# A depthwise convolution that reads its rows from PSUM, its halo through ScalarE's bias, and norm rows transposed at other places

## The chip, the core and the metric

The kernel runs on one core of a Trainium2 chip. Five engines work beside each other: TensorE (PE, with its weight loads shown as PEld), VectorE (DVE), ScalarE (ACT), GpSimd (POOL), and SyncE (SP), which here issues the DMAs. The metric is the device time of one execution in microseconds. Before the change three runs took 3058.79, 3064.16 and 3069.94 us; the median is 3064.16.

## The reference

One "macaron" block over x of 4 x 1024 tokens and 512 channels, all in float32: half a feed-forward layer, a Mamba mixer, half a feed-forward layer. Each of the three reads a layer norm of the running x.

```python
x = x + 0.5 * ffn(layernorm(x))          # (silu(g*gate_s) * (u*up_s)) @ down.T * down_s, 1408 wide
x = x + mixer(layernorm(x))
x = x + 0.5 * ffn(layernorm(x))

# the mixer: 1024 inner channels, 16 states, a convolution of 4 taps
h, gate = split(x @ W_in.T)
h = silu(causal_depthwise_conv4(h) + conv_b)
ts, B, C = split(h @ Wx.T)               # 128 + 16 + 16 columns, each with an rms norm
delta = softplus(ts @ Wdt.T + dt_bias)
s_t = exp(delta_t * A) * s_(t-1) + delta_t * B_t * u_t       # scan over time, u = h
y = (s_t . C_t + D * u) * silu(gate)
out = y @ Wout.T
```

## The kernel before

The 4096 tokens are cut into eight chunks of 512; two chunks make a sequence of 1024, so an odd chunk continues the even one before it and needs its last three columns (the halo) for the convolution. A chunk goes through stages: `ffn1`, `prep_in` (input projection, convolution, gates, x projection), `dt0` to `dt3` (each two of eight channel tiles of delta), `post` (gating and output projection) and `ffn2`. Beside them `scan` runs 32 groups a chunk, each of a GpSimd product (line 1020), four exponentials on ScalarE into PSUM (1034), four scans on VectorE (1043), 16 transposes on TensorE (1060) and four accumulations, on VectorE (1071) or through ScalarE and GpSimd (1075, 1078).

Float32 products run in split form (`hi` and `lo` parts, `PARTS`): three products for each, or two where the weight has no `lo` part. The program holds both forms of the feed-forward weights' order and picks one by a flag that it works out at the start; with these ternary weights the shorter one runs. A stage begins with `make_xT`, which transposes the 512 x 512 norm rows, loaded by DMA into `xnb`, through four PSUM banks into `xT`; ScalarE writes `hi` (527) and VectorE `lo` (528). PSUM has four banks `pm` for all stages, two `pa` for the exponentials, two `pt` for the scan's transposes.

In `prep_in` each of the eight channel tiles has a product of 12 matmuls (505) into a bank. ScalarE copies it into a row of `xnb` (738), behind three halo columns (736, odd chunks), and writes the last tap with bias to `a` (740); in even chunks it saves the last three columns (745). VectorE adds the three other taps (750), ScalarE takes the tanh (700), VectorE makes u (701), ScalarE its `hi` (704), GpSimd its `lo` (706). Two tiles are open at a time: a tile's 700 to 706 are issued behind the taps of the next. A gate product (12 matmuls, ScalarE tanh 785, VectorE 787) stands between. Two of the four banks are held from the start for the x projection, of which 12 matmuls (`x_step`, 720) follow each tile with a lag of two. `x_proj` then normalises the result on ScalarE and GpSimd, and `dt0` transposes it.

The order of stages is a table: `OPENING` for the first, then `ROUND` for each chunk, where `LAG` = 3 puts `post` and `ffn2` three chunks later. No engine's order is written by hand. Each stage issues into streams ("threads": M for stages, C for the convolution, D for softplus, S and T for the scan, L for norms); `merge` (from line 114) plays all streams against a cost model (`span`: for VectorE 0.09 + n/960 us, and the `more` that an operation gives) with ranks by engine, and takes at each step the instruction that can start first. The result is a fixed order on each engine, and an instruction waits on semaphores in that order. Softplus works in three buffers, `spx`, `spe`, `spw`, which one part must leave (918 and the stores) before the next part's biased copy (882) may write.

## Time and profile before

| | |
|---|---|
| profiled execution, its own time | 3060.28 us |
| its span, first to last instruction | 3058.5 us |
| busy: TensorE, VectorE, ScalarE, GpSimd | 80%, 85%, 58%, 75% of the span |
| granted TensorE clock, mean | 0.885 |
| first and last scan start | 205.7 and 2939.0 us |
| VectorE taps of the convolution (750) | 192 instructions |
| VectorE's last step of the convolution (701) | 64 instructions |

The shares are means over stages with different limits, so the stretch of the scans and single stages are read beside them. A duration in the trace holds whatever an instruction waits for after its issue; an idle gap before it is listed apart with what ended it. Lines in the rows are those of the kernel before.

### The profile page before, as it was taken

Reading aid. Unit: us, or ns where it says so; the run is one execution under the profiler, and the core shown is the slowest. Engines: PE = TensorE matmul, PEld = TensorE weight load, DVE = VectorE, ACT = ScalarE, POOL = GpSimd, SP = SyncE. Lnnn points to the kernel's source line nnn. Section 1 sums busy time; section 2 is a strip of 40 time slices with the busy share of each in tenths; the row PEclk is TensorE's granted clock in tenths of the full one; section 3 lists DMA queues with packets and bytes.
Section 4 is the critical chain, followed back from the end, with each engine's and each line's share of the span. In section 5 each row is a group of like instructions: output and inputs, shape, how many; then the busy total and the mean of one; then the engine's idle time right before and its main releaser. Section 6 shows DMA issues by size and latency. Waiting matters only on the chain. (4 is left out here: it accounts for less than half of the span.)

```text
span 3058.5 us, 37435 instructions
## 1 busy us (share of the span) xinstructions
PE 2454.4 (80%) x12266; PEld 1985.8 (65%) x12266; DVE 2595.8 (85%) x3097; ACT 1778.5 (58%) x3029; POOL 2288.8 (75%) x1348
## 2 busy tenths in 40 slices
PE   7568786876878899779987899778988897697768
PEld 5456565655657678567766677667766675576646
DVE  5449897999899889799998899899998897899962
ACT  5456557666646656657665656646656656745421
POOL 2237758886986689768996789858897698997832
PEclk9778797988888899889989999889989897897879
DMA  7544653564376566865577466855677475575624
GB/s 271 198 160 137 198 195 90 176 226 160 128 265 233 170 208 220 290 206 171 187 258 285 145 203 221 272 191 172 208 238 274 132 238 191 194 250 191 199 79 133
DMA packets 294953, 608.70 MB, mean 199 GB/s; under 512 B 23008, under 2 KB 23776, under 8 KB 294752
## 3 DMA queue, kind: packets, MB, share of 16 engines
q1 hardware_dynamic: 294752, 606.23, 59.8%
q8 instruction: 101, 1.65, 0.2%
q14 instruction: 100, 0.82, 0.1%
HBM read 453.57 MB, written 152.57 MB: 198 GB/s over the span
## 5 line engine op out<-in xcount | busy, mean ns | idle before, releaser
L1020 POOL TENSOR_TENSOR sbuf<-dus,bring 128x1024 f32<-128x1024 f32 x512 | 1236.0, 2430 | 271.1 <-PE pt L1060 150.2
L505 PE MATMUL pm<-xT,wring 128*128 128x512 f32 x4352 | 1144.9, 412 | 92.3 <-DVE xT L528 48.7
L505 PEld LDWEIGHTS pm<-xT,wring 128*128 128x128 f32 x4352 | 825.2, 196 | 263.1 <-issue 92.9
L1034 ACT ACTIVATE pa<-dls,cst 128x512 f32<-128x512 f32 x1024 | 692.0, 688 | 475.4 <-DVE sbuf L1043 453.9
L1060 PE MATMUL pt<-ident,sbuf 128*128 128x128 f32 x4096 | 688.2, 309 | 314.6 <-DVE sbuf L1043 188.9
L1060 PEld LDWEIGHTS pt<-ident,sbuf 128*128 128x128 f32 x4096 | 538.4, 158 | 484.4 <-DVE sbuf L1043 242.0
L1043 DVE TENSOR_TENSOR_SCAN sbuf<-pa,carry,sbuf 128x512 f32<-128x512 f32 x512 | 634.4, 1270 | 37.4 <-ACT pa L1034 23.7
L1043 DVE TENSOR_TENSOR_SCAN sbuf<-pa,sbuf 128x512 f32<-128x512 f32 x512 | 607.4, 1211 | 65.8 <-ACT pa L1034 58.3
L1071 DVE SCALAR_TENSOR_TENSOR acc<-pt,cT,acc 128x512 f32<-128x512 f32 x768 | 548.6, 742 | 98.6 <-PE pt L1060 86.3
L577 PE MATMUL pm<-wring,act 128*128 128x512 f32 x2176 | 589.1, 414 | 32.6 <-DVE hd L957 23.4
L577 PEld LDWEIGHTS pm<-wring,act 128*128 128x128 f32 x2176 | 405.5, 195 | 122.9 <-DVE hd L957 26.6
L528 POOL TENSOR_TENSOR act<-hd,act 128x512 fp32r<-128x512 f32 x240 | 310.3, 1299 | 105.5 <-ACT act L527 104.9
L1078 POOL TENSOR_TENSOR acc<-acc,tmp 128x512 f32<-128x512 f32 x192 | 253.1, 1318 | 72.7 <-ACT tmp L1075 72.6
L640 ACT ACTIVATE th<-pm,csh 128x512 f32<-128x512 f32 x176 | 120.5, 685 | 160.4 <-PE pm L505 159.9
L706 POOL TENSOR_TENSOR act<-hd,act 128x512 fp32r<-128x512 f32 x64 | 82.2, 1284 | 154.1 <-ACT act L704 151.5
L750 DVE SCALAR_TENSOR_TENSOR aa<-xnb,csh,aa 128x511 f32<-128x511 f32 (+1 forms) x144 | 179.8, 1249 | 16.2 <-ACT aa L740 15.2
L527 ACT ACTIVATE act<-hd 128x512 fp32r<-128x512 f32 x240 | 148.8, 623 | 56.6 <-DVE hd L957 40.9
L1075 ACT ACTIVATE tmp<-pt,cT 128x512 f32<-128x512 f32 x192 | 131.2, 683 | 66.4 <-POOL acc L1078 59.2
L644 DVE SCALAR_TENSOR_TENSOR aa<-th,pm 128x512 f32<-128x512 f32 x176 | 118.3, 672 | 53.0 <-ACT th L640 52.4
L720 PE MATMUL pm<-wxs,act 128*128 128x160 f32 x768 | 121.1, 312 | 51.5 <-POOL act L706 37.3
L720 PEld LDWEIGHTS pm<-wxs,act 128*128 128x128 f32 x768 | 113.7, 226 | 61.0 <-issue 22.5
L652 DVE SCALAR_TENSOR_TENSOR hd<-aa,csh,pm 128x512 f32<-128x512 f32 x176 | 129.7, 737 | 14.3 <-PE pm L505 11.5
(121 smaller groups left out, 2106.5 us busy)
## 6 DMA issues: line engine op xcount, KB each, us to landing
wring<-wsp SPq DMA_DIRECT2D x408, 512.0 KB, 4.4
bring<-b_d SPq DMA_DIRECT2D x256, 256.0 KB, 3.9
xn_d<-tb SPq DMA_DIRECT2D x24, 1024.0 KB, 8.9
xnb<-xn_d SPq DMA_DIRECT2D x21, 1024.0 KB, 6.5
x_d<-tb SPq DMA_DIRECT2D x16, 1024.0 KB, 5.8
u_d<-hd SPq DMA_DIRECT2D x64, 256.0 KB, 2.3
sg_d<-hd SPq DMA_DIRECT2D x64, 256.0 KB, 2.9
tb<-x_d SPq DMA_DIRECT2D x16, 1024.0 KB, 6.7
```

What stands on the lines that cost most here:

```text
L505: f = lambda e, pw=pw, px=px, k=k, first=(i == 1), end=(i == total): e.matmul(pm[b][:, 0:n], lhs(pw, k), rhs(px, k), start=first, stop=end)
L527: t_hi = M.op(hi_eng, lambda e: e.activation(hi, b_or_src, ACT.Copy), t_src, *waits)
L528: t_lo = M.op(lo_eng, lambda e: e.tensor_tensor(lo, b_or_src, hi, ALU.subtract), t_hi)
L577: f = lambda e, b=b, pw=pw + half, px=px, k=k, tt=tt, slot=slot, start=(i and k == 0), stop=(end and k == nk - 1): e.matmul(pm[b][:, :], a ...
L720: f = lambda e, b=b, tt=tt, pw=pw, px=px, start=first_here, stop=(end and k == NI - 1): e.matmul(pm[b][:, (tt % 2) * XW:(tt % 2 + 1) * XW] ...
L750: t_c = C.op("dve", lambda e, xb=xb, a=a, k=k, lo=lo, cw=cw: e.scalar_tensor_tensor(a[:, lo:TC], xb[:, HALO - k + lo:HALO - k + TC], cw(3 ...
L1020: t_p = S.op("pool", lambda e, s2=s2, s3=s3, h=h: e.tensor_tensor(sbuf[:, s3, h * m:(h + 1) * m, :], dus[:, h * m:(h + 1) * m, :], bring[: ...
L1034: t_e = S.op("act", lambda e, k=k, i=i, pb=pb, n=n: e.activation(pa[pb][:, :], dls[:, k, :], ACT.Exp, scale=col(C_A + i * N + n)), dl_tok[ ...
L1043: t_sc = S.op("dve", lambda e, d=d, pb=pb, init=init: e.tensor_tensor_scan(d, pa[pb][:, :], d, init, ALU.mult, ALU.add), t_e, t_ps[k], *(s ...
L1060: f = lambda e, tt=tt, k=k, s3=s3, pb=pb: e.matmul(pt[pb][:, k * P:(k + 1) * P], sbuf[:, s3, k, tt * P:(tt + 1) * P], ident[:, :], is_tran ...
L1071: f = lambda e, tt=tt, a=a, c=c, pb=pb, n=n: e.scalar_tensor_tensor(a, pt[pb][:, :], cT[:, c % 4, tt, n:n + 1], a, ALU.mult, ALU.add)
L1078: t_a = T.op("pool", lambda e, a=a: e.tensor_tensor(a, a, tmp[:, 0, :], ALU.add), t_s, *w)
```

## The change

Names and tables first. `ROUND` has `dt2` in front of `post` and `dt3` in front of `prep_in`; `INSIDE` puts `dt1` into the middle of `ffn1`; `EARLY` names the stages that transpose the next stage's rows.

```diff
+EARLY = ("ffn","prep_in")
+D_ACT = 5
+CLOSE_NOW = tuple(range(8))
+INSIDE = (("ffn1", "dt1"),)
+TWO_OPEN = (0,)
+WITH_CONV = (0,)
-ROUND = (("ffn1",0),("dt1",1),("post",LAG),("dt2",1),("prep_in",0),("dt3",1),("ffn2",LAG),("dt0",0))
+ROUND = (("ffn1",0),("dt1",1),("dt2",1),("post",LAG),("dt3",1),("prep_in",0),("ffn2",LAG),("dt0",0))
```

Chunk 0 keeps rows in `xnb` (`rows`), two open tiles and x steps between tiles. Chunks 1 to 7 leave the product in its bank: the taps read the bank at a shifted start, and the tanh goes back into it. The halo's part of the first three columns of an odd chunk, with the convolution's bias, is worked out for all tiles by six small GpSimd products and sums (`hfix`), and enters as the bias of three ScalarE activations of one column. Each tile is finished before the next is issued.

```diff
+                if not even:
+                    cw4 = csh[:, H_CW:H_CW + 4 * NI].rearrange("p (i k) -> p i k", k=4)
+                    at = {3: 0, 2: 4, 1: 6}
+                    for k in (3, 2, 1):
+                        t_fix = C.op("pool", lambda e, k=k: e.tensor_tensor(
+                            hfix[:, :, at[k]:at[k] + k], hsave[:, :, HALO - k:HALO],
+                            cw4[:, :, 3 - k:4 - k].broadcast_to([P, NI, k]), ALU.mult),
+                            *(hs_tok if k == 3 else ()), *freed("hfix"), n=8)
...
-                    t_th = C.op("act", lambda e: e.activation(xb[:, HALO:HALO + TC], a, ACT.Tanh), t_c, table="tanh")
+                    h = x_buf[i % 3] if rows else pm[b][:, :]
+                    t_th = C.op("act", lambda e: e.activation(h, a, ACT.Tanh), t_c, table="tanh")
                     t_u = C.op("dve", lambda e: e.scalar_tensor_tensor(
-                        hd[:, r, :], xb[:, HALO:HALO + TC], 1.0, a, ALU.add, ALU.mult), t_th, *freed(("hd", r)))
+                        hd[:, r, :], h, 1.0, a, ALU.add, ALU.mult), t_th, *freed(("hd", r)), more=0.2 if rows else 0.0)
...
+                    x = x_buf[i % 3] if rows else pm[b][:, :]
+                    if rows:
+                        C.op("act", lambda e, b=b, x=x: e.activation(x, pm[b][:, :], ACT.Copy), t, *x_free[i % 3])
                     if even:
...
+                        hs_tok[i] = C.op("dve", lambda e, b=b, i=i: e.tensor_copy(
+                            hsave[:, i, 0:HALO], pm[b][:, TC - HALO:TC]), t_c, *freed("hsave"), n=1)
+                    else:
+                        for k in range(HALO):
+                            C.op("act", lambda e, b=b, a=a, i=i, k=k, cw=cw: e.activation(
+                                a[:, k:k + 1], pm[b][:, k:k + 1], ACT.Identity, bias=hfix[:, i, k:k + 1],
+                                scale=cw(3)), t, t_fix, *freed(a_key[i % 3]), n=40)
+                        t_c = C.op("act", lambda e, b=b, a=a, i=i, cw=cw: e.activation(
+                            a[:, HALO:TC], pm[b][:, HALO:TC], ACT.Identity, bias=hc(H_CB + i), scale=cw(3)),
+                            t, more=0.1)
...
                     for k in range(1, 4):
-                        lo = k if even else 0
-                        t_c = C.op("dve", lambda e, xb=xb, a=a, k=k, lo=lo, cw=cw: e.scalar_tensor_tensor(
-                            a[:, lo:TC], xb[:, HALO - k + lo:HALO - k + TC], cw(3 - k), a[:, lo:TC], ALU.mult, ALU.add),
-                            t_c, more=0.06)
+                        t_c = C.op("dve", lambda e, x=x, a=a, k=k, cw=cw: e.scalar_tensor_tensor(
+                            a[:, k:TC], x[:, 0:TC - k], cw(3 - k), a[:, k:TC], ALU.mult, ALU.add),
+                            t_c, more=0.3 if rows else 0.06)
                     if opened:
                         finish()
-                    opened.append((i, r, t_c))
+                    opened.append((i, r, b, t_c))
+                    if c not in TWO_OPEN:
+                        finish()
```

In chunks 1 to 7 the banks of the x projection are taken behind the last gate, seven x steps follow, then the next stage's transposes, then the last x step and `x_proj`. `ffn` calls `next_xT` in front of its down-projection; it acts where the next stage but the dt parts is one whose norm rows are stored by then, and loads and transposes them.

```diff
+            def next_xT(where):
+
+                key = following[0]
+                if where in EARLY and key in ln_out:
+                    need_xn(key)
+                    early_xT[key] = make_xT(xn_tok.pop(key))
+                    prefetch()
...
+                    if j == J // 2 and within:
+                        within()
                 finish()
                 free["xT"] = (t,)
+                if not first:
+                    next_xT("ffn")
...
+                if c not in WITH_CONV:
+                    x_banks()
+                for k in range(NI - XLAG if c in WITH_CONV else 0, NI - 1):
                     x_step(k)
-                free["act"] = (x_done[-1][1],)
-                x_proj(c, x_done)
+
+                if c:
+                    next_xT("prep_in")
+
+                def close():
+                    x_step(NI - 1)
+                    free["act"] = (x_done[-1][1],)
+                    x_proj(c, x_done)
+
+                to_close.append(close)
+                if c in CLOSE_NOW:
+                    close_x()
```

Three places show how the orders move. Lines in the pieces of the change are its own: 809 for 750, 766 for 701, 869 for 787, 1127 for 1043, 1155 for 1071, 743 for 720, 512 for 505, 520 for 513, 584 for 577, 1144 for 1060. A scan stands as SCALAR_TENSOR_TENSOR `sbuf<-pa`.

VectorE in `prep_in` of chunk 5, from the taps of one tile to the last step of another, before:

```order
L750 SCALAR_TENSOR_TENSOR th<-xnb,csh,th 128x512 x2
L1071 SCALAR_TENSOR_TENSOR acc<-pt,cT,acc 128x512
L750 SCALAR_TENSOR_TENSOR th<-xnb,csh,th 128x512
L701 SCALAR_TENSOR_TENSOR hd<-xnb,aa 128x512
L1071 SCALAR_TENSOR_TENSOR acc<-pt,cT,acc 128x512 x2
L1043 SCALAR_TENSOR_TENSOR sbuf<-pa,sbuf 128x512
L787 SCALAR_TENSOR_TENSOR hd<-th,pm 128x512
```

and of the change, one tile:

```order
L809 SCALAR_TENSOR_TENSOR th<-pm,csh,th 128x511
L869 SCALAR_TENSOR_TENSOR hd<-th,pm 128x512
L809 SCALAR_TENSOR_TENSOR th<-pm,csh,th 128x510
L1127 SCALAR_TENSOR_TENSOR sbuf<-pa,sbuf 128x512
L809 SCALAR_TENSOR_TENSOR th<-pm,csh,th 128x509
L1127 SCALAR_TENSOR_TENSOR sbuf<-pa,sbuf 128x512 x2
L766 SCALAR_TENSOR_TENSOR hd<-pm,th 128x512
L1127 SCALAR_TENSOR_TENSOR sbuf<-pa,sbuf 128x512
```

Before, a tile's last step (701, on `aa`) stands behind the three taps of the next tile (on `th`); now it stands behind its own, with scans between, and its first tensor is the bank `pm`.

TensorE at the end of `prep_in` of chunk 5, where `xT,wring` are the last gate products, `wxs` the x projection, `tsT` dt parts and `ident,xnb` the transposes of the next stage, `ffn2`, before:

```order
L1060 MATMUL pt<-ident,sbuf 128x128 x8
L505 MATMUL pm<-xT,wring 128x512 x6
L1060 MATMUL pt<-ident,sbuf 128x128 x4
L505 MATMUL pm<-xT,wring 128x512
L1060 MATMUL pt<-ident,sbuf 128x128 x4
L720 MATMUL pm<-wxs,act 128x160 x24
L1060 MATMUL pt<-ident,sbuf 128x128 x12
L505 MATMUL pm<-tsT,wdts 128x512
L1060 MATMUL pt<-ident,sbuf 128x128 x4
L505 MATMUL pm<-tsT,wdts 128x512 x5
L513 MATMUL pm<-ident,xnb 128x128 x16
L505 MATMUL pm<-xT,wring 128x512 x9
```

and of the change:

```order
L743 MATMUL pm<-wxs,act 128x160 x6
L1144 MATMUL pt<-ident,sbuf 128x128 x4
L743 MATMUL pm<-wxs,act 128x160
L1144 MATMUL pt<-ident,sbuf 128x128 x4
L743 MATMUL pm<-wxs,act 128x160 x44
L520 MATMUL pm<-ident,xnb 128x128 x2
L1144 MATMUL pt<-ident,sbuf 128x128 x8
L520 MATMUL pm<-ident,xnb 128x128 x6
L1144 MATMUL pt<-ident,sbuf 128x128 x8
L520 MATMUL pm<-ident,xnb 128x128 x8
L743 MATMUL pm<-wxs,act 128x160 x12
L512 MATMUL pm<-xT,wring 128x512 x3
```

The x projection stood in twelves between the products and now stands behind them in one piece; the transposes moved in front of its last twelve and the first product of `ffn2` follows these.

TensorE at the end of `ffn2` of chunk 2 (`wring,act` is the down-projection, `ident,ssb` and `tsT` are `dt0`), before:

```order
L1060 MATMUL pt<-ident,sbuf 128x128 x4
L577 MATMUL pm<-wring,act 128x512 x17
L513 MATMUL pm<-ident,ssb 128x128 x4
L513 MATMUL pm<-ident,bn 128x128
L1060 MATMUL pt<-ident,sbuf 128x128 x8
L505 MATMUL pm<-tsT,wdts 128x512 x3
L1060 MATMUL pt<-ident,sbuf 128x128 x4
L505 MATMUL pm<-tsT,wdts 128x512
L1060 MATMUL pt<-ident,sbuf 128x128 x4
L505 MATMUL pm<-tsT,wdts 128x512 x2
L513 MATMUL pm<-ident,xnb 128x128 x16
L505 MATMUL pm<-xT,wring 128x512 x10
```

and of the change:

```order
L512 MATMUL pm<-xT,wring 128x512 x4
L520 MATMUL pm<-ident,xnb 128x128 x2
L1144 MATMUL pt<-ident,sbuf 128x128 x4
L520 MATMUL pm<-ident,xnb 128x128 x2
L1144 MATMUL pt<-ident,sbuf 128x128 x4
L520 MATMUL pm<-ident,xnb 128x128 x12
L584 MATMUL pm<-wring,act 128x512 x20
L1144 MATMUL pt<-ident,sbuf 128x128 x8
```

The 16 transposes of `ffn1`'s rows stood behind `dt0`, right in front of the products that need them; they now stand in front of the down-projection.

## Rows read from the trace of the kernel before

**Rows 1.** the page, busy time by engine, share of the span, instructions

```profile
PE 2454.4 (80%) x12266; PEld 1985.8 (65%) x12266; DVE 2595.8 (85%) x3097; ACT 1778.5 (58%) x3029; POOL 2288.8 (75%) x1348
```

**Rows 2.** windows: us, busy PE, PEld, DVE, ACT, POOL, PEclk, DMA share, GB/s

```profile
230.00:2945.00 2715.00, 2212.28 (x11235) 1787.66 (x11235) 2449.86 (x2842) 1643.73 (x2788) 2198.29 (x1267) 0.89 0.61 201
```

**Rows 3.** windows of one round's ffn1 and prep_in

```profile
1132.50:1218.80 86.30, 81.78 (x437) 67.22 (x437) 80.27 (x96) 55.94 (x95) 81.75 (x47) 1.00 0.63 207
...
1271.20:1386.30 115.10, 91.08 (x472) 75.63 (x471) 106.20 (x120) 74.85 (x143) 79.80 (x47) 0.89 0.63 207
```

**Rows 4.** waits: engine, line, releaser: us in total, times, longest

```profile
ACT act L704 <- DVE hd L701: 119.9, 48, 8.7
...
DVE acc L1071 <- PE pt L1060: 86.3, 89, 5.4
...
PE pm L505 <- DVE xT L528: 48.7, 21, 4.7
...
PE pm L505 <- DVE hd L787: 33.1, 12, 7.9
```

**Rows 5.** groups by line on VectorE: busy us, mean ns, idle before

```profile
L1071 DVE SCALAR_TENSOR_TENSOR acc<-pt,cT,acc 128x512 f32<-128x512 f32 x768 | 548.6, 742 | 98.6 <-PE pt L1060 86.3 <-POOL acc L1078 6.8 <-ACT acc L1067 0.8
...
L750 DVE SCALAR_TENSOR_TENSOR aa<-xnb,csh,aa 128x511 f32<-128x511 f32 (+1 forms) x144 | 179.8, 1249 | 16.2 <-ACT aa L740 15.2
...
L750 DVE SCALAR_TENSOR_TENSOR th<-xnb,csh,th 128x512 f32<-128x512 f32 (+3 forms) x48 | 57.5, 1198 | 8.2 <-ACT th L740 7.7
...
L701 DVE SCALAR_TENSOR_TENSOR hd<-xnb,aa 128x512 f32<-128x512 f32 x48 | 51.3, 1068 | 1.3 <-ACT xnb L700 1.2
...
L787 DVE SCALAR_TENSOR_TENSOR hd<-th,pm 128x512 f32<-128x512 f32 x64 | 42.9, 670 | 15.9 <-DMA sg_d<-hd 10.9 <-ACT th L785 4.8
...
L701 DVE SCALAR_TENSOR_TENSOR hd<-xnb,th 128x512 f32<-128x512 f32 x16 | 15.2, 951 | 0.0
```

**Rows 6.** lines 750 and 1071: duration ns min/median/max

```profile
L750 DVE SCALAR_TENSOR_TENSOR aa<-xnb,csh,aa x144: 718/752/2927, 110.6 to 2401.8; 128x512 f32<-128x512 f32 x72, 128x511 f32<-128x511 f32 x24, 128x510 f32<-128x510 f32 x24, 128x509 f32<-128x509 f32 x24
...
L1071 DVE SCALAR_TENSOR_TENSOR acc<-pt,cT,acc x768: 717/743/758, 232.2 to 2944.3; 128x512 f32<-128x512 f32 x192
```

**Rows 7.** timeline of GpSimd: start us, us

```profile
1359.08 2.37 POOL L1020 TENSOR_TENSOR sbuf<-dus,bring 128x1024 f32<-128x1024 f32 x1
```

**Rows 8.** timeline of VectorE beside it

```profile
1359.28 2.71 DVE L750 SCALAR_TENSOR_TENSOR aa<-xnb,csh,aa 128x511 f32<-128x511 f32 x1
1361.92 1.27 DVE L1043 TENSOR_TENSOR_SCAN sbuf<-pa,carry,sbuf 128x512 f32<-128x512 f32 x1
1363.11 0.72 DVE L750 SCALAR_TENSOR_TENSOR aa<-xnb,csh,aa 128x510 f32<-128x510 f32 x1
```

**Rows 9.** groups by line on ScalarE and GpSimd

```profile
L738 ACT ACTIVATE xnb<-pm 128x512 f32<-128x512 f32 x64 | 37.4, 584 | 15.1 <-PE pm L505 15.1
L740 ACT ACTIVATE aa<-pm,csh 128x512 f32<-128x512 f32 x48 | 37.0, 771 | 0.0
...
L736 ACT ACTIVATE xnb<-hsave 128x3 f32<-128x3 f32 x32 | 6.2, 194 | 0.0
...
L825 POOL TENSOR_TENSOR cT<-ssb,rr 128x64 f32<-128x64 f32 x8 | 2.4, 298 | 0.0
```

**Rows 10.** timeline of TensorE, two x steps

```profile
1041.24 2.81 PE L720 MATMUL pm<-wxs,act 128*128 128x160 f32 x24
```

**Rows 11.** timeline of ScalarE, dt0 and ffn1, then one tile in prep_in

```profile
1137.87 0.67 ACT L882 ACTIVATE spx<-pm,cst 128x512 f32<-128x512 f32 x1
...
1166.78 0.67 ACT L640 ACTIVATE th<-pm,csh 128x512 f32<-128x512 f32 x1
...
1288.24 0.76 ACT L740 ACTIVATE aa<-pm,csh 128x512 f32<-128x512 f32 x1
...
1304.86 0.63 ACT L704 ACTIVATE act<-hd 128x512 fp32r<-128x512 f32 x1 [5.49 <-DVE hd L701]
```

**Rows 12.** timeline of GpSimd, dt0's last product

```profile
1169.25 2.40 POOL L918 TENSOR_TENSOR spw<-spx,spw 128x1024 f32<-128x1024 f32 x1
```

More of the change, by code:

```diff
@@ L240, in macaron @@
         hsave = sb("hsave", [P, NI, 4])
+        hfix = sb("hfix", [P, NI, 8])
         cst = sb("cst", [P, NCONST])
@@ L680, in prep_in @@
                 even = c % 2 == 0
-                src, t_in = (tb, first_xn[-1]) if c == 0 else (xnb, xn_tok.pop((1, c)))
-                t_xT = make_xT(t_in, src)
+                t_xT = ready_xT((1, c)) if c else make_xT(first_xn[-1], tb)
                 if c + 1 < NCH:
                     pre_norm(free, ln_out, c + 1)
+                if c == 0 and c not in WITH_CONV:
+                    prefetch(0)
                 u_tok, g_tok = [], []
-                opened, x_ready_of = [], {}
-                xbanks = [bank() for h in range(2)]
@@ new lines, in prep_in, with x_banks, x_step @@
+                opened, x_ready_of, x_done, xbanks = [], {}, [], []
+                def x_banks():
+                    xbanks.extend(bank() for h in range(2))
+                    held.update(b for b, w in xbanks)
+                def x_step(k):
+                    for tt in range(4):
+                        b, w = xbanks[tt // 2]
+                        for pw, px in PARTS:
+                            begins, ends = (pw, px) == PARTS[0], (pw, px) == PARTS[-1]
+                            opens = begins and k == 0 and tt % 2 == 0
+                            f = lambda e, b=b, tt=tt, pw=pw, px=px, start=opens, stop=(ends and k == NI - 1): e.matmul(
+                                pm[b][:, (tt % 2) * XW:(tt % 2 + 1) * XW], act[:, pw, k, tt * P:(tt + 1) * P],
+                                wxs[:, px, k, :], start=start, stop=stop, skip_group_check=True)
+                            ws = (*x_ready_of[k], t_small[0]) if begins and tt == 0 else ()
+                            t = M.matmul(f, *ws, *(w if opens else ()), n=XW, last=ends and tt % 2 == 1)
+                            if ends and k == NI - 1 and tt % 2 == 1:
+                                x_done.append((b, t))
@@ L711, in finish @@
                     x_ready_of[i] = t_hi, t_lo
[L713 to L728 removed]
                 for i in range(NI):
[L730 removed]
+                    r, a = i % 2, a_buf[i % 3]
                     slot, t_w = piece(WIN + i)
@@ L762, in prep_in @@
-                prefetch(0 if c == 0 else 1)
+                if opened:
+                    finish()
+                if rows:
+                    free["xnb"] = tuple(t for f in x_free for t in f)
+                    prefetch(0)
                 if c:
@@ L839, in dt0 @@
             def dt0(c):
+                close_x()
                 t_bn, t_ct, t_ss = bn_tok[c]
@@ L1169, in build @@
                     scan(c)
-                if kind in KIND and (kind, c) not in INPLACE:
+                if kind in KIND and (kind, c) not in INPLACE and (KIND[kind], c) not in early_xT:
                     need_xn((KIND[kind], c))
-                stage[kind](c)
+                later = [x for x in order[order.index((kind, c)) + 1:] if x[0][:2] != "dt"]
+                following[0] = None
+                if later and later[0][0] in KIND and later[0] not in INPLACE:
+                    following[0] = KIND[later[0][0]], later[0][1]
+                more = [lambda k=k, n=n: stage[k](n) for k, n in [inner.get((kind, c))] if k] if (kind, c) in inner else []
+                stage[kind](c, *more)
         build(True, True)
```

91 lines of the change are left out of this document (49 added, 42 removed).

## The prediction, made before the changed kernel was run

> **What bounds the kernel now.** I read five views, from wide to narrow. First the busy times: VectorE leads with 2595.8 us of the span, TensorE and GpSimd follow at 80% and 75% [rows 1]. Then the long middle stretch alone, from 230 us to 2945 us, in which the scans run: VectorE is busy 2449.86 us of 2715, that is 90.2%, GpSimd 2198.29 (81.0%), TensorE 2212.28 (81.5%), ScalarE 61% [rows 2]. VectorE's idle time there is 265 us. Third, two stages of one round of the main chain: in ffn1 TensorE is busy 81.78 of 86.3 us, but in prep_in VectorE is busy 106.20 of 115.1 us and TensorE only 91.08 [rows 3]. So ffn stages are close to TensorE's limit, and prep_in, the one the change rewrites, is close to VectorE's. Fourth, the waits: ScalarE's operand split waits 119.9 us for VectorE's last convolution step, and the accumulation behind the scan waits 86.3 us for TensorE [rows 4]. Last the instruction groups of the convolution: they run on VectorE at 1249, 1198, 1068 and 951 ns, while a like instruction with its first tensor in PSUM takes 670 to 742 ns [rows 5, 6].
>
> Why they differ is seen in one pair of rows. A GpSimd product runs from 1359.08 to 1361.45 [rows 7]; a VectorE convolution step issued at 1359.28 takes 2.71 us and ends at 1361.99, half a microsecond after it, where the next one, with GpSimd idle, takes 0.72 [rows 8]. The spread over the whole run says the same: least 718, median 752, longest 2927 ns; the accumulation that reads PSUM stays between 717 and 758 in 768 executions [rows 6]. The step reads two SBUF tensors, the accumulation one.
>
> **The change part by part.** The profiled execution took 3060.28 us, 1.8 us more than its span, and lies 3.9 us under the median of the runs shown; I count from 3060.
>
> *Convolution out of PSUM (chunks 1 to 7).* 192 steps of L750 cost 179.8 + 57.5 = 237.3 us [rows 5]; seven eighths of them, 168, cost 207.6. At the 742 ns of L1071, which has the same operands (PSUM tensor, scalar column, SBUF tensor), they cost 124.7: 82.9 us less. L701's 64 cost 51.3 + 15.2 = 66.5; 56 of them 58.2; at the 670 ns of L787 [rows 5] 37.5: 20.7 less. The 32 saves of the last three columns move from ScalarE to VectorE; for so small a copy the nearest row is ScalarE's 194 ns for three columns [rows 9]: 6.2 us more. VectorE loses 97 us of work. Bounds for the new steps: 717 to 758 ns [rows 6], so 95 to 102.
>
> That the bank is now read several times has a rule against it: the Trainium skill ("VectorE: DVE Perf Modes", "Rules for kernel authors") advises copying a matmul's result to SBUF first when many operations follow, and its errata table charges 120 cycles for a PSUM source against 58 for SBUF. By that each of the 224 operations would cost 65 ns more, 14.5 us in all (an estimate from that page). The trace does not bear it out: the least times are 717 ns with PSUM and 718 without [rows 6].
>
> *ScalarE.* 56 copies of L738 go (584 ns, 32.7 us), with 32 halo copies (6.2) and the 32 saves; 96 one-column activations come, at the 194 ns of the three-column copy [rows 9] 18.6 us. At least 20 us less on an engine that is busy 61% of the stretch: worth nothing by itself. GpSimd gets 24 tiny products for the halo, at most 8 us at the 298 ns of the kernel's 64-element products [rows 9], ahead of the convolution and in its gaps: nothing.
>
> *Banks and order in prep_in.* Two of the four pm banks no longer are held for the x projection while tiles run, so conv and gate products rotate over four; TensorE's 33.1 us of waits for L787 [rows 4], which frees a gate's bank, shrink. Against it, a bank is held through the tile's whole chain, and each tile is finished before the next begins: the overlap of two open tiles goes. All x steps stand behind the last tile. 24 of them took 2.81 us [rows 10], so 96 take 11.2 us at the end of the stage, 84 in one run and 12 behind the next stage's transposes, with VectorE left to the scans.
>
> *Norm rows early.* A stage's first product waits for the split of its transposed rows: 48.7 us in 21 waits, 2.3 each [rows 4]. The change does this early at the end of prep_in for chunks 1 to 7 and in front of the down-projection of ffn2 for four chunks: 11 starts, 25 us of TensorE waits at most. Its waits are half filled by other streams, so none to 25.
>
> *dt1 inside ffn1 (five rounds).* Its biased copy L882 may not overwrite spx before dt0's L918 has read it. dt0's copy began at 1137.87 and L918 ended at 1169.25 + 2.40 = 1171.65; ffn1's sixth tanh, behind which dt1 now stands, began at 1166.78 [rows 11, 12], and its product is done some 3 us later. With the stage's start 3 us earlier the wait is 0 to 5 us, ScalarE's queue behind it (the scan's exponentials) waiting too: 0 to 25 us in five rounds, I take 10.
>
> *The sum.* What does 97 us less on VectorE give? If its 265 us of idle time stay as they are, 97. The idle time should grow a little: TensorE's work is unchanged, and its 2212 us would then be 84.5% of 2618. The scans fill VectorE whenever they are free to, as the stretch shows, and at the end of the kernel little else is left for it; the shorter prep_in lets them run ahead of the main chain. I take 80%, 78 us, and add 12 for the early transposes (half of 25) less 10 for dt1: 80 us. 3060 - 80 = **2980 us**. Own range of this case: 70% to 110% of 97 with the ends of the other terms, 2950 to 3015.
>
> **The rivals.** *TensorE and GpSimd take over:* the gain of prep_in returns as waits in the ffn stages, where TensorE is at 81.78 of 86.3 [rows 3]. Only prep_in's own idle can be won: its 115.1 us cannot fall below TensorE's 91, and other stages grow by the scan work pushed into them. A third of the 97 remains: 3060 - 32 = 3028. For it: TensorE's 81.5%. Against: no engine but VectorE passes 82% over the stretch.
>
> *More than the sum:* waits go together with work (prep_in's copies, the bank waits, 48.7 us of split waits), and idle falls below 265 by a third of the split and bank waits' 82 us and a few more: 97 + 33, 2930. For it: the convolution's 2 us stalls are not foreseen by the planner, whose price for a step is 0.09 + 512/960 + 0.06 = 0.68 us (line 73 and the `more` of line 750), and the new 0.74 fits it.
>
> *Slower, by the tile's chain:* one tile at a time costs the biased copy 0.77 [rows 9] + three columns 0.6 + three steps 2.23 + tanh 0.63, as the split [rows 11] + last step 0.67 + split 0.63 = 5.5 us; if each of the four VectorE steps finds a scan (1.27 [rows 8]) and an accumulation (0.74) in front, 8 more, and six handovers 1: 14.5 us. Eight tiles and the x run are 127 us against 115.1, five to seven times: 12 x 7 = 84 us on the main chain; 3060 + 84 - 25 = about 3120. It decides from 13 us a tile on. For it: the first tile's copy began at 1288.24 and its split only at 1304.86, 16.6 us later [rows 11]. Against: much of that was the second tile's work queued between.
>
> *No change:* the excess over 0.72 us is not the second SBUF tensor's, and stays. Then only the small terms act, +10 to -15: 3055. Against it: [rows 6 to 8]. By the page's table above (the Trainium skill, "VectorE: DVE Perf Modes") 14.5 would come on top.
>
> **How the numbers follow.** Less than 0.3%, 9 us, cannot be told from no change: the three runs differ by 11. Forecast 56%, take-over 19%, more 12%, slower 8%, no change 5%. The range 2925 to 3045 holds the first two and most of the third, 84%. Faster: 56 + 19 + 12, less 1 for the edge of the take-over: 86%. Same 6%, slower 8%.
>
> **What would show it.** The steps and L701's successor at 740 and 670 ns with no tail past 800; VectorE near 2500 us; prep_in at 95 to 105 us; waits of the split for the last step nearly gone; waits for xT under 25 us. Wrong: steps still in the microsecond, a prep_in over 115 us, L882 waiting for L918 by several us a round, or VectorE lighter by 97 us with the span unmoved.

## The result, and the profile after

The changed kernel took 3032.21 us (median of 4 runs, 3031.36 to 3035.97), the kernel before 3063.3 beside it: a ratio of 0.9899, 95% interval 0.9883 to 0.9914. It is 31 us faster; 80 were forecast.

The page of the kernel after, busy time by engine as in [rows 1]; then the taps of the convolution on VectorE and its last step, least, median and longest duration, as in [rows 6]:

```profile
PE 2454.4 (81%) x12266; PEld 1988.6 (66%) x12266; DVE 2487.0 (82%) x3129; ACT 1769.5 (58%) x3005; POOL 2262.2 (75%) x1372
```

```profile
L809 DVE SCALAR_TENSOR_TENSOR aa<-pm,csh,aa x126: 718/737/751, 378.8 to 2411.6; 128x511 f32<-128x511 f32 x42, 128x510 f32<-128x510 f32 x42, 128x509 f32<-128x509 f32 x42
L809 DVE SCALAR_TENSOR_TENSOR th<-pm,csh,th x42: 719/734/750, 400.8 to 2392.9; 128x511 f32<-128x511 f32 x14, 128x510 f32<-128x510 f32 x14, 128x509 f32<-128x509 f32 x14
L766 DVE SCALAR_TENSOR_TENSOR hd<-pm,aa x42: 657/667/692, 385.5 to 2414.5; 128x512 f32<-128x512 f32 x42
L766 DVE SCALAR_TENSOR_TENSOR hd<-pm,th x14: 660/666/683, 406.4 to 2395.5; 128x512 f32<-128x512 f32 x14
```

The work went as priced: 2595.8 to 2487.0 is 108.8 us less on VectorE (97 forecast), the taps stand at 734 to 737 ns with nothing past 751, the last step at 667. The time did not follow. Windows of the middle stretch, and of one round's ffn1 and prep_in (us, busy PE, PEld, DVE, ACT, POOL, then clock, DMA share, GB/s), answering to [rows 2, 3]:

```profile
230.00:2915.00 2685.00, 2214.79 (x11247) 1792.92 (x11247) 2341.00 (x2866) 1634.88 (x2772) 2168.64 (x1283) 0.89 0.60 202
...
1155.80:1242.60 86.80, 79.99 (x395) 64.04 (x394) 64.42 (x79) 55.34 (x85) 71.93 (x42) 0.98 0.73 249
1298.00:1415.60 117.60, 93.89 (x503) 77.10 (x501) 109.88 (x150) 74.33 (x116) 84.97 (x58) 0.88 0.63 211
```

The two stages are bounded as in [rows 3]: ffn1 from the transposes of dt0 to its last product, prep_in from the dt part in front of it to its last product or transpose. VectorE now idles 344 us of the stretch (265 of a like one before). prep_in takes 117.6 us, where 95 to 105 were expected and over 115 was to be the sign of being wrong, and VectorE is 93% busy in it (92% before). ffn1 is as long as before (86.3), with TensorE busy 79.99 us of it, and VectorE has fallen from 80.27 to 64.42. The scans alone in the same two windows (us, busy VectorE, count), before and after, show where they went, from ffn1 into prep_in:

```profile
1132.50:1218.80 86.30, 45.23 (x38) 1.00 0.63 207
1271.20:1386.30 115.10, 45.29 (x37) 0.89 0.63 207
```

```profile
1155.80:1242.60 86.80, 32.32 (x27) 0.98 0.73 249
1298.00:1415.60 117.60, 53.62 (x43) 0.88 0.63 211
```

The waits, as in [rows 4], two of the kernel before that stand in no row yet, then those of the kernel after:

```profile
POOL sbuf L1020 <- PE pt L1060: 150.2, 58, 8.5
...
DVE sbuf L1043 <- POOL sbuf L1020: 20.2, 8, 5.8
```

```profile
POOL sbuf L1104 <- PE pt L1144: 229.2, 81, 9.5
...
DVE sbuf L1127 <- POOL sbuf L1104: 73.7, 30, 8.8
...
PE pm L512 <- DVE xT L535: 30.4, 13, 3.8
...
ACT act L773 <- DVE hd L766: 21.8, 16, 2.5
```

ScalarE's split waits 21.8 us for the last step (119.9 before), but the scan's own loop waits more: GpSimd's product 229.2 us for TensorE's transposes (150.2 before), and VectorE's scan 73.7 for that product (20.2).

What ended last has changed too. VectorE's timeline (start, duration) at the last scan, before and after, and beside them pieces of the chain of work that ended last:

```profile
2939.05 1.27 DVE L1043 TENSOR_TENSOR_SCAN sbuf<-pa,carry,sbuf 128x512 f32<-128x512 f32 x1
...
2939.13 1.20 DVE sbuf L1043
2940.38 3.09 PE pt L1060 x12
```

```profile
2894.40 2.45 DVE L1127 TENSOR_TENSOR_SCAN sbuf<-pa,carry,sbuf 128x512 f32<-128x512 f32 x2
...
2900.03 7.99 PE pm L584 x35
...
2908.40 4.43 DMA act<-u_d
...
2914.11 8.40 DMA act<-u_d
...
2924.14 18.01 PE pm L584 x78
```

The scans end 43 us earlier, the kernel only 29 us earlier in its span: behind the last scan stood 118 us (3058.5 - 2940.3), just the last half of post and the last ffn2; now it is 133. Before, the chain runs through the last scan and its transposes: the stages waited for the scans at the end. After, it runs from a down-projection (584) over loads of post into the last ffn2, past the scans: the stages are late by themselves, by some 15 us. This stretch behind the last scan tells the two cases apart in every run: it is 117 to 119 us where the scans end last (before, e1 to e4, e7, e10, e12, e13, e15 to e17) and 133 to 176 where the stages do (after, e5, e6, e8, e9, e11, e14, e18).

From the first scan to the end of the last, before and after, the columns of the windows above:

```profile
205.69:2940.32 2734.63, 2223.32 (x11267) 1795.96 (x11267) 2460.89 (x2852) 1654.87 (x2806) 2214.29 (x1273) 0.89 0.61 201
```

```profile
207.15:2896.85 2689.70, 2213.18 (x11211) 1790.51 (x11212) 2344.14 (x2864) 1643.56 (x2786) 2176.31 (x1283) 0.89 0.60 201
```

VectorE has 117 us less to do there and idles 72 us more. The scans have come closer to their data, too. GpSimd's last product of dt1 and the first of the scan, chunk 7, before and after:

```profile
2576.94 2.40 POOL L918 TENSOR_TENSOR spw<-spx,spw 128x1024 f32<-128x1024 f32 x1
...
2670.95 4.77 POOL L1020 TENSOR_TENSOR sbuf<-dus,bring 128x1024 f32<-128x1024 f32 x2 [1.57 <-DMA dus<-du_d]
```

```profile
2575.99 2.36 POOL L1001 TENSOR_TENSOR spw<-spx,spw 128x1024 f32<-128x1024 f32 x1
...
2610.77 4.65 POOL L1104 TENSOR_TENSOR sbuf<-dus,bring 128x1024 f32<-128x1024 f32 x2 [4.68 <-DMA dus<-du_d]
```

The scan starts 92 us behind its data before, 32 after.

The seven tile sections of prep_in (first tap of a chunk to its last, chunks 1 to 7) say why. Each "sum" row gives their length and the busy times over them, the second one that of the scans alone. Before:

```profile
sum 554.00, PE 433.44 PEld 354.83 DVE 527.71 ACT 308.13 POOL 357.01; mean PE 61.92 PEld 50.69 DVE 75.39 ACT 44.02 POOL 51.00
...
sum 554.00, DVE 180.28; mean DVE 25.75
```

After:

```profile
sum 537.90, PE 422.66 PEld 330.21 DVE 496.42 ACT 339.65 POOL 396.76; mean PE 60.38 PEld 47.17 DVE 70.92 ACT 48.52 POOL 56.68
...
sum 537.90, DVE 228.54; mean DVE 32.65
```

VectorE lost 104 us of convolution here, but its busy time fell only by 31: scans (48 us more) and their accumulations (25 more) took the room. The sections hardly got shorter, 76.9 us each instead of 79.1. VectorE's timeline in one tile after shows how:

```profile
1354.80 0.74 DVE L809 SCALAR_TENSOR_TENSOR aa<-pm,csh,aa 128x511 f32<-128x511 f32 x1
1355.46 1.27 DVE L1127 TENSOR_TENSOR_SCAN sbuf<-pa,carry,sbuf 128x512 f32<-128x512 f32 x1
1356.65 0.73 DVE L809 SCALAR_TENSOR_TENSOR aa<-pm,csh,aa 128x510 f32<-128x510 f32 x1
1357.29 1.27 DVE L1127 TENSOR_TENSOR_SCAN sbuf<-pa,carry,sbuf 128x512 f32<-128x512 f32 x1
1358.48 0.72 DVE L809 SCALAR_TENSOR_TENSOR aa<-pm,csh,aa 128x509 f32<-128x509 f32 x1
```

A scan stands behind each of the first two taps. The timeline has 112 pairs of neighbouring taps of one tile in chunks 1 to 7: 11 stand side by side, and between the others are 58 scans, 35 accumulations and some steps of the stages.

### The profile page after: what moved, and what is told of

Same layout as the page of the kernel before. It is cut to its first block and busy times, and to the rows that moved or that the text cites. A ratio compares the mean times of both kernels' runs of the same rounds, so it can differ in the third digit from the quotient of the medians.

```text
span 3029.6 us, 37464 instructions
## 1 busy us (share of the span) xinstructions
PE 2454.4 (81%) x12266; PEld 1988.6 (66%) x12266; DVE 2487.0 (82%) x3129; ACT 1769.5 (58%) x3005; POOL 2262.2 (75%) x1372
## 5 line engine op out<-in xcount | busy, mean ns | idle before, releaser
L1104 POOL TENSOR_TENSOR sbuf<-dus,bring 128x1024 f32<-128x1024 f32 x512 | 1219.1, 2395 | 314.6 <-PE pt L1144 229.2
L512 PE MATMUL pm<-xT,wring 128*128 128x512 f32 x4352 | 1132.5, 409 | 89.2 <-DVE xT L535 30.4
L1144 PE MATMUL pt<-ident,sbuf 128*128 128x128 f32 x4096 | 678.3, 306 | 263.4 <-DVE sbuf L1127 154.2
L1144 PEld LDWEIGHTS pt<-ident,sbuf 128*128 128x128 f32 x4096 | 532.1, 157 | 424.4 <-DVE sbuf L1127 204.5
L600 POOL TENSOR_TENSOR tb<-tb 128x512 f32<-128x512 f32 x64 | 80.7, 1294 | 64.5 <-DVE tb L598 64.5
```

What stands on the lines that cost most here:

```text
L512: f = lambda e, pw=pw, px=px, k=k, first=(i == 1), end=(i == total): e.matmul(pm[b][:, 0:n], lhs(pw, k), rhs(px, k), start=first, stop=end)
L1104: t_p = S.op("pool", lambda e, s2=s2, s3=s3, h=h: e.tensor_tensor(sbuf[:, s3, h * m:(h + 1) * m, :], dus[:, h * m:(h + 1) * m, :], bring[: ...
L1144: f = lambda e, tt=tt, k=k, s3=s3, pb=pb: e.matmul(pt[pb][:, k * P:(k + 1) * P], sbuf[:, s3, k, tt * P:(tt + 1) * P], ident[:, :], is_tran ...
```

## The experiments

Theory M: two chains, the stages and the scans, share VectorE in one fixed order; the end is set by the later, and the gain is only what that one gets. Rivals: T, TensorE and GpSimd are the limit of the ffn stages; S, the scans wait for their data; O, accidents of the planner's order. All are the changed kernel with the edit shown, unless said otherwise.

**Parts undone, and who gives way.**

e1, the convolution from SBUF rows in all chunks, two tiles open, the x projection's banks held and its steps between the tiles as before; the rest of the change stays. The lines left out place the loads of norm rows and free the banks to suit.

```diff
-TWO_OPEN = (0,)
-WITH_CONV = (0,)
+TWO_OPEN = tuple(range(8))
+WITH_CONV = tuple(range(8))
...
```

> The changed kernel with the convolution of all chunks out of SBUF rows again, two tiles open and x steps between the tiles; early transposes, halo bias and dt order stay. Theory M (main chain): the freed VectorE time of the change went to scan steps between a tile's taps, so the chain of stages got no shorter, and now it, no longer the scan, ends last. VectorE gets back about 100 us; the scan ends last again: 3050 to 3065 us. Theory T (TensorE and GpSimd at their throughput): the PSUM form is worth about its third, 30 us: also 3050 to 3065. If the PSUM form is worth nothing and early transposes and dt order made the whole gain: 3030 to 3038.

3060.38 us, ratio 0.9997 (0.998 to 1.0015): with VectorE at 2593.5 us again, nothing is left of the gain. M and T had named the same range, so the run does not part them. The new order of dt and the early rows are in it, and together are worth nothing beside SBUF rows.

e2, dt1 to dt3 at their old places.

```diff
-INSIDE = (("ffn1", "dt1"),)
+INSIDE = ()
-ROUND = (("ffn1",0),("dt1",1),("dt2",1),("post",LAG),("dt3",1),("prep_in",0),("ffn2",LAG),("dt0",0))
+ROUND = (("ffn1",0),("dt1",1),("post",LAG),("dt2",1),("prep_in",0),("dt3",1),("ffn2",LAG),("dt0",0))
```

> The changed kernel with the table of stages of before (post between dt1 and dt2, dt3 behind prep_in) and dt1 not inside ffn1. M: a scan's data come 20 to 50 us later a chunk, but post follows with no dt work in front; as the stages end last, 3005 to 3030 us, with the first post behind the last prep_in 15 to 30 us earlier. If the scan's supply is what counts: 3045 to 3065. T: no change, 3027 to 3037.

3054.93 us, 0.998 (0.996 to 1.0). VectorE has the light load (2478.5), yet 23 us are lost. M's 3005 to 3030 is missed, and the rival that the scan's supply counts (3045 to 3065) is right. GpSimd's waits in this run show that the scan stands for its data (43.4 us in the kernel after, 71.5 before):

```profile
POOL sbuf L1104 <- DMA dus<-du_d: 99.5, 18, 14.6
```

So the order of dt1 to dt3, of which I had priced dt1 alone, at a loss of 10, is a gain of 23 beside PSUM.

e3, two tiles open in all chunks, everything else as changed.

```diff
-TWO_OPEN = (0,)
+TWO_OPEN = tuple(range(8))
```

> The changed kernel with two convolution tiles open in all chunks (a tile's tanh and last step issued behind the next tile's taps), still out of PSUM. M: the tile section of prep_in falls from 76 to 80 us to 65 to 72, and the time by 10 to 40 us: 2992 to 3022. T: no change, 3027 to 3037. If the tile's own chain is not what holds prep_in but VectorE's queue: section and time unchanged too.

3008.79 us, 0.9827 (0.9809 to 0.9845), a time within what M said: one tile at a time costs 23 us. But M's reason is not borne out: a section takes 75.5 us, not 65 to 72. The scans end last again, 6 us earlier than as changed, and the stretch behind them is 117 us instead of 133.

e4, scans and accumulations give way to the stages on VectorE.

```diff
-"t": dict(pe=0, dve=3, ...  "s": dict(act=4, dve=4,
+"t": dict(pe=0, dve=50, ... "s": dict(act=4, dve=60,
```

> The changed kernel with a handicap in the planner: on VectorE a scan is placed only where it can start 0.6 us before any other work that is ready, an accumulation 0.5 us (ranks 60 and 50 in place of 4 and 3). Same instructions, other order. M: taps follow each other without scans between, the tile section falls from 76 to 80 us to about 60 and the time by 30 to 70 us: 2960 to 3000. T: TensorE's and GpSimd's work is the same, so 3025 to 3040 whatever prep_in does.

3072.81 us, 1.0037 (1.0023 to 1.0051): slower, M's and T's numbers missed. The sections are what the forecast had wanted:

```profile
sum 418.70, PE 353.13 PEld 282.01 DVE 363.52 ACT 272.87 POOL 278.19; mean PE 50.45 PEld 40.29 DVE 51.93 ACT 38.98 POOL 39.74
...
sum 418.70, DVE 123.73; mean DVE 17.68
```

59.8 us a section. The last chunk's prep_in begins at 2195.9 us instead of 2336.1, but the scans left undone end last:

```profile
2959.15 1.28 DVE L1127 TENSOR_TENSOR_SCAN sbuf<-pa,carry,sbuf 128x512 f32<-128x512 f32 x1
```

**Which chain is late.**

e5, no early transposes: `EARLY = ()`.

> The changed kernel with EARLY = (): every stage transposes its own rows at its start, as before. The prediction's price (half of 25 us): 3032 + 12 = 3044 us, waits of TensorE for xT back at 45 to 50 us. Theory M (two chains, the stages and the scans, share VectorE in a fixed order, and the end is set by the later of the two; behind the change the stages are the later one by some 15 us): the wait lies on the later chain, 3038 to 3050. Theory T (TensorE and GpSimd are the limit of the ffn stages, VectorE's gain is lost there): a wait of TensorE counts in full, 3045 to 3057.

3035.37 us, 0.9897 (0.9881 to 0.9914), close to the change's own 0.9899: the early rows are worth 3 us or nothing; all three numbers missed. TensorE's waits for xT, expected at 45 to 50 us, rose from 30.4 only to 34.4, so the run takes little of them back.

e6, from chunk 2 on the scan reads the chunk before's delta, delta*u, B and C.

```diff
-                d_tok, (t_b,), t_ct = scan_ready[c]
+                d = c - 1 if c > 1 else c
+                d_tok, (t_b,), t_ct = scan_ready[d]
...
-dls[:, k, :], dl_d[c, 4 * ig + k]
+dls[:, k, :], dl_d[d, 4 * ig + k]
...
```

> The changed kernel, but from chunk 2 on the scan reads delta, delta*u, B and C of the chunk before, so it never waits for this chunk's softplus; all work and all traffic stay, only the numbers differ. Theory S (the shorter convolution has let the scans catch up with their data, and now they wait for softplus: scan(7) starts 29 us behind its data, 117 before the change): the scans end at least 30 us earlier and the time is 2985 to 3015 us. Theory M: the scans end earlier, but they stand in front of the stages' steps on VectorE, and the stages end last: 3020 to 3045. Theory T: 3025 to 3035, nothing moves.

3025.56 us, 0.9865 (0.9846 to 0.9884). The last scan:

```profile
2846.89 1.27 DVE L1128 TENSOR_TENSOR_SCAN sbuf<-pa,carry,sbuf 128x512 f32<-128x512 f32 x1
```

The scans end 49 us earlier and the kernel is 7 us faster. So the scans did wait for their data, as S says, but S's time falls: behind the change the stages are the later chain, as M says. (T's number holds the time too, but not that the scans move. The 29 and 117 us in the expectation are not counted from the same dt part; from dt1 they are the 32 and 92 above.)

e7, one tap less in chunks 1 to 7, and e8, one accumulation of 16 less; each takes 56 steps of 0.74 us, 41 us, from VectorE.

```diff
-                    for k in range(1, 4):
+                    for k in range(1, 4 if rows else 3):
```

```diff
+                        elif n == 7 and c:
+                            t_s = t_a = t_t
```

> The changed kernel without the tap of the oldest column in chunks 1 to 7: 56 VectorE steps of 0.74 us, 41 us, all of them in the chain of a tile in prep_in (the convolution has three taps instead of four). The prediction's rate (80 %): 3032 - 33 = 2999. Theory M: the step lies on the later chain, and each of its steps waits behind a scan besides; the end can fall until the scans end last, 15 us, and by half of what they gain beyond: 3000 to 3018. Theory T: 3024 to 3032.

> The changed kernel without the accumulation of state 7 behind the scans of chunks 1 to 7: 56 VectorE steps of 0.74 us, 41 us, as much as the tap, but spread over all stages and not in a tile's chain (the sum over the states lacks one of 16; its transposes stay). The prediction's rate (80 %): 2999. Theory M: the stages end last and gain only by the places that come free in VectorE's order, 3012 to 3027. Theory T: 3024 to 3032.

e7: 2974.03 us, 0.9686 (0.9665 to 0.9708); e8: 3051.58 us, 0.9957 (0.994 to 0.9973). The same relief of VectorE (2447.0 and 2450.5 us) gives 58 us in the tile's chain and a loss of 19 in the scans. A section of e7 takes 63.9 us, 13 less for 8 steps of 0.74: with each step goes what stands in front of it. In e7 the scans end 40 us earlier than as changed and last again; in e8 they end when they did, and the stages 12 us later. Both miss all numbers; that the tap is worth more than the accumulation is M's, the loss in e8 is not, and at 19 us it is little more than an accident of order (below).

**The corners, and the size of accidents.**

e9, one tile at a time from SBUF rows (e1 with `TWO_OPEN = (0,)`).

> The convolution of all chunks from SBUF rows as in e1, but with one tile at a time in chunks 1 to 7 (two open in chunk 0 alone); halo through the bias, early rows and the order of dt as changed. With the changed kernel (PSUM, one tile: 3032), e3 (PSUM, two open: 3009) and e1 (SBUF, two open: 3060) this is the fourth corner. Theory M (the change traded the overlap of two tiles for shorter steps, and the one nearly paid for the other in prep_in): a tile's chain gets longer by three steps' excess of 0.5 us, eight tiles, seven stages, 84 us, less what VectorE was idle: 3080 to 3110. Theory O (the order that the planner happens to find moves the time by some 20 us whatever is changed, and e3's gain is that): 3050 to 3075, no dearer than e1. Theory T: 3060 to 3070.

3142.76 us, 1.0249 (1.0226 to 1.0271): 82 us over e1, and 33 past M's range; O's range is far off. Sections of 95.6 us:

```profile
sum 669.30, PE 511.25 PEld 424.17 DVE 624.23 ACT 370.61 POOL 441.12; mean PE 73.04 PEld 60.60 DVE 89.17 ACT 52.94 POOL 63.02
```

e10, e2 and e3 together: two tiles open, dt at its old places.

> Two tiles open in all chunks, convolution from PSUM, but dt1 to dt3 at their old places. Theory M (gain only where the stages and the scans get shorter together): with the scans waiting for their data again (99.5 us of waits for du in e2) nothing of e3's 23 us is left, 3045 to 3060. Theory O: the two add up or not by chance, 3015 to 3060. Theory T: two open tiles ease TensorE's waits, 3030 to 3035.

3029.93 us, 0.9881 (0.9858 to 0.9903). M is wrong here: two open tiles are worth 25 us also without the new order of dt (23 with it), and that order 21 also with two open tiles. With PSUM the two terms add. They do not add with the rows: PSUM instead of SBUF rows is worth 51 us with two tiles open (e1 to e3) and 111 with one (e9 to the change), in each case together with the x projection's move.

e11 and e12, a nudge: the planner's allowance behind a VectorE instruction 0.14 instead of 0.13 us, on the changed kernel and on e3.

```diff
-LATE = {"pe": 0.3, "act": 0.13, "dve": 0.13, "pool": 0.15}
+LATE = {"pe": 0.3, "act": 0.13, "dve": 0.14, "pool": 0.15}
```

> The changed kernel; only the planner's allowance behind a VectorE instruction is 0.14 us instead of 0.13, so that the same instructions with the same sizes stand in another order on each engine. Theory M: the time is set by the chains and stays within 6 us of 3032. Theory O: it moves by 10 to 25 us, either way.

> The same nudge (0.14 instead of 0.13) with two tiles open in all chunks. Theory M: within 6 us of 3009. Theory O: 10 to 25 us off, and the lead of two open tiles over one (23 us) shrinks or grows by as much.

3017.69 us, 0.9844 (0.9814 to 0.9874), and 3011.84, 0.9824 (0.9803 to 0.9846): 14 us less and 3 more, for the same work. O is right for the first, M for the second. In this pair one tile at a time costs only 6 us.

e13, the same nudge on the kernel before; e14, `PEF = 1.11` instead of 1.12 on the changed kernel.

> The kernel before with the planner's allowance behind a VectorE instruction at 0.14 us instead of 0.13: same instructions, another order. The nudge moved the changed kernel by 14 us and the one with two open tiles by 3. Theory O (order accidents of 10 to 25 us in every form): 3040 to 3090, more than 9 us off 3064. Theory M (before the change the scans end last and follow their chain): 3058 to 3070.

> The changed kernel with the planner's price of a matmul at 1.11 instead of 1.12 of its rate: again only the order moves. Theory O: 3005 to 3045, at least 8 us from both 3032 and 3018 or on either side of them. Theory M (stages last, 3032 an ordinary draw): 3025 to 3040. A value of 3010 to 3022 would say that 3032 was an unlucky order, and that one tile at a time costs nearer 8 us than 23.

3051.44 us, 0.995 (0.9934 to 0.9967), and 3028.79, 0.9862 (0.9837 to 0.9887). The order alone moves the kernel before by 14 us too, as O said; e14 moves by 3, within M's range. Two of four nudges thus gave 14 us and two gave 3. Single executions of one kernel scatter besides, the four of e14 from 3016 to 3039. A difference of under 15 us between two orders of this program cannot be told from such an accident.

**Does the filling lose the gain?**

e15, e4's edit with milder ranks, 13 and 20 instead of 50 and 60; e16, the same with two tiles open.

> The changed kernel with scans and their accumulations ranked behind the stages' steps on VectorE by 0.2 and 0.13 us (e4: 0.6 and 0.5; as changed: 0.04 and 0.03). Theory M (VectorE is 92% busy in a tile section of prep_in in every form; what its steps give up is filled with scans, 27 instead of 20, and the section keeps its 75 us; e4 brought it to 60 us with 15 scans, and the scans ended last): between the two, section at 65 to 72 us, both chains ending nearer to each other, 3005 to 3025 us. Theory T: 3025 to 3040.

> The same milder ranks with two tiles open in all chunks. Theory M: in e3 both chains already end within some 10 us of each other, so little is left: 2990 to 3010. Theory O: 3000 to 3030 by chance. Theory T: 3005 to 3015.

e15: 2996.82 us, 0.9776 (0.9749 to 0.9802), 35 us under the change, the fastest with all the work, and 8 below M's range; e16: 3015.07, 0.9832 (0.9816 to 0.9849), past M's range and in O's. In e15 a section takes 64.6 us with fewer scans than before the change, 65 of the 112 pairs of taps stand side by side and no scan stands in a pair, and the scans end last again, but early (118 us before the end of its span of 2992.5):

```profile
sum 452.60, PE 371.54 PEld 293.41 DVE 404.65 ACT 290.59 POOL 305.13; mean PE 53.08 PEld 41.92 DVE 57.81 ACT 41.51 POOL 43.59
...
sum 452.60, DVE 155.79; mean DVE 22.26
```

```profile
1282.47 1.53 DVE L809 SCALAR_TENSOR_TENSOR aa<-pm,csh,aa 128x511 f32<-128x511 f32 x2
1284.66 0.75 DVE L1155 SCALAR_TENSOR_TENSOR acc<-pt,cT,acc 128x512 f32<-128x512 f32 x1 [0.65 <-PE pt L1144]
1285.32 0.74 DVE L809 SCALAR_TENSOR_TENSOR aa<-pm,csh,aa 128x509 f32<-128x509 f32 x1
...
2873.25 1.27 DVE L1127 TENSOR_TENSOR_SCAN sbuf<-pa,carry,sbuf 128x512 f32<-128x512 f32 x1
```

e17, the ranks of e15 in the kernel before; e18, ranks 8 and 12 in the changed one.

> The kernel before with the ranks of e15 (scans 20, their accumulations 13, on VectorE). e15 took 2997 us where the changed kernel takes 3032, so the control is what the ranks alone are worth. Theory M (before the change the scans end last, 88 us or more behind their data, so giving way takes from the later chain): the section of prep_in gets shorter and the scans end later, 3060 to 3095. Rival R (the ranks are worth 35 us in either kernel and have nothing to do with the change): 3020 to 3040.

> The changed kernel with scans at 12 and accumulations at 8, between the changed kernel (4, 3) and e15 (20, 13). In e15 the scans end last again and post(7)'s first half stands 80 us before them, so the best share lies between. Theory M: section 67 to 73 us, 2985 to 3010. Theory O (accidents of the order): anywhere from 2990 to 3030.

e17: 3076.86 us, 1.0048 (1.0032 to 1.0065), 13 us slower than before and within M's range, with sections of 75.4 us instead of 79.1 and scans that end 12 us later. There the scans were the later chain. The 13 us alone could be an accident; that the ranks by themselves do not give 35 us is clear, and R falls. e18: 3029.36, 0.9884 (0.9863 to 0.9906): no gain, M missed, O's range holds it. Its sections are 75.1 us, and 15 of 112 pairs of taps stand side by side (11 as changed, 65 in e15, 103 in e4). The planner's lines account for it:

```python
LATE = {"pe": 0.3, "act": 0.13, "dve": 0.13, "pool": 0.15}
...
                cost += 0.01 * rank.get(eng, 9)
...
            end += LATE[eng]
```

To the planner a tap is ready 0.13 us after the one before it, 0.14 with its own rank; whatever waits ready goes in between if its rank costs less. Scans at 0.04 and 0.12 do, at 0.20 they don't; accumulations at 0.03 to 0.13 do (35 between the pairs as changed, 32 in e15), at 0.50 they don't (none in e4). It is a step at 0.14, not a share.

The gap itself is there on the chip. Two taps together took 1.53 us, the second of them 0.75, so it started 0.78 us after the first (the median of 65 pairs in e15); an instruction that does not need the tap's result started 0.66 us after it (1354.80 to 1355.46 above). What costs the tile is the size of what goes in: for a gap of 0.13 us a scan of 1.27 is let in, and from tap to tap it is then 1.85 us (1354.80 to 1356.65) instead of 0.78. VectorE wins the 0.13 and the tile's chain loses over 1 us.

## Why the prediction was wrong

*Price of the steps: right.* VectorE lost 108.8 us for 97, the taps stand at 734 to 737 ns for 742, the last step at 667 for 670, and most of ScalarE's wait for the last step went. The excess lies in the share of seven eighths: chunk 0's 24 taps took only 17.9 us of the 237.3, so that chunks 1 to 7 had more to lose. That a PSUM source is not dearer, argued from the least times, held (below). The rival "no change" is out. The low end of the range does not come out of its own terms: 110% of 97 with 25 for the early rows and nothing for dt1 is 3060 - 107 - 25 = 2928, not 2950.

*"I take 80%": the step that failed.* It let VectorE's idle time grow only "a little". Between the first and the last scan VectorE has 117 us less work and 72 us more idle time, so the scans end only 43 us earlier, and behind them the stages end 15 us later than they would if they waited for scans alone. The sentence "the shorter prep_in lets them run ahead of the main chain" took for granted that prep_in gets shorter. It did not: the planner puts scans and accumulations that are ready between the dependent steps of a tile, so freed time turns into more scans in the same section and fewer in ffn1, and a tile's chain grows by them. The scans also came closer to their data (32 us behind it, 92 before), and in e6, freed of that wait, they end 49 us earlier. I had read VectorE's 106.20 of 115.1 us in prep_in [rows 3] as the weight of its steps there; a third of VectorE's time in the tile sections were scans already (180.28 of 527.71 us). e15 keeps the scans out of the gaps, and 35 of the 52 us between 3032 and 2980 come back; e17 shows that the same ranks gain nothing in the kernel before. The ranks act in all stages, so that the whole of the 35 us is prep_in's is not shown.

*"The overlap of two open tiles goes", cost left out.* It stood as a rival of 14.5 us a tile, and nothing of it in the sum. With SBUF rows it is 82 us (e1 to e9), with PSUM 23 or 25, 6 in the nudged pair. The rival's mechanism acted, its price was too high: a tile takes 9.6 us of a section. It had put a scan and an accumulation, 2.0 us, in front of every step; between two taps stand 0.9 us of them on average (58 and 35 in 112 pairs).

*dt1 inside ffn1: -10 forecast; dt1 to dt3 together +21 to +23 with PSUM.* I counted the wait of its biased copy for GpSimd's product; it is 5.4 us in 5 waits:

```profile
ACT spx L965 <- POOL spw L1001: 5.4, 5, 2.0
```

I did not count what an earlier dt gives: the scan's data (99.5 us of waits in e2, 43.4 as changed). The moves of dt2 and dt3 were not priced at all, and no run moves dt1 alone, so its own share stays open.

*Early rows: +12 forecast, 3 measured, within the noise.* TensorE's waits for xT fell from 48.7 to 30.4, but e5, without the early rows, has 34.4: most of the fall is not theirs.

*The sum as measured* depends on the path. By e10 and e2 it is 35 for PSUM, less 25 for one tile at a time, and 23 for dt; by e1 and e3 it is 3 for dt and early rows, 51 for PSUM, less 23. Either adds up to 31 to 33 because it runs from the same start to the same end, so that the sum fits proves nothing, and each term carries an accident of up to 15.

*The take-over rival* named 3028, near the 3032 found, and its picture of ffn1 is right: TensorE is busy 79.99 of 86.8 us there, and VectorE's gain turns up as idle time. As the bound of the kernel it is not borne out: e15 and e7 are 35 and 58 us faster with TensorE's work unchanged. That it came close is luck.

The Trainium skill ("Perfetto Trace Analysis", "Identifying the Most-Contended Engine") says to take the engine with the highest occupancy first. VectorE it was, and 41 us off it gave 58 us in one place (e7) and a loss in another (e8): here the place decided.

Open: why VectorE idles 10 to 14% of the time between the first and the last scan in the runs looked at, what e8's 19 us are beyond an accident, and why two open tiles no longer help under e15's ranks. That the scan's loop (product, scan, transposes) sets the idle time was not tried.

## What to carry to other kernels

When an engine serves two chains in a fixed order, ask of each freed microsecond which chain the scheduler hands it to, and which of the two ends last; look at what stands between the steps of one chain, not at the engine's share. Compare the gap that the scheduler fills with the length of what it puts there: a gap of 0.13 us, real as it was, drew in scans of 1.27 us. And nudge the scheduler without changing the work before trusting a difference: here that alone was up to 14 us.

## What the runs showed of the hardware

A tap with both tensors in SBUF has a least time like that from PSUM and a long tail beside GpSimd. In e1:

```profile
L810 DVE SCALAR_TENSOR_TENSOR aa<-xnb,csh,aa x144: 717/750/3003, 111.2 to 2395.0; 128x511 f32<-128x511 f32 x48, 128x510 f32<-128x510 f32 x48, 128x509 f32<-128x509 f32 x48
```

717 to 3003 ns there, 718 to 751 from PSUM in the kernel after. All 74 taps of e1 that took over 0.8 us ran beside a GpSimd instruction; so did 126 of the 168 taps from PSUM, and none of these passed 751. The Trainium skill ("SBUF — State Buffer", "Who interferes with whom") says that a VectorE instruction with two SBUF inputs contends with a GpSimd one that reads SBUF; the trace agrees. The table of the Trainium skill in "VectorE: DVE Perf Modes" (the errata section), 120 cycles for a PSUM source against 58, is not seen: 718 against 717.

A tap that needs the result of the tap before it started 0.78 us behind that one's start, an instruction that does not need it 0.66 us (medians in e15): the dependence cost some 0.13 us.
